# Layer norm's two small operations moved from GpSimd to VectorE, with six reorderings in a fused attention and FFN kernel

## What is computed

```
xn = layernorm(x)
q, k, v = xn @ Wq.T, xn @ Wk.T, xn @ Wv.T        # 16 heads of 16
q, k    = q / |q|, k / |k|                       # per head
p       = softmax(q k.T - slope_h * |distance|)  # only the next 127 keys and the own one
s       = (p v) @ Wo.T
gate    = fp4(xn) @ fp4(w_gate).T                # 256 -> 704; fp4 in blocks of 16
h       = silu(gate) * (fp4(xn) @ fp4(w_up).T)
g       = silu(fp4(h) @ fp4(w_down).T)           # 704 -> 256
out     = x + s * g
```

## Time and profile before

| | us |
|---|---|
| median of three runs | 502.65 |
| the profiled execution | 503.14 |
| its span in the profile | 501.4 |
| TensorE busy | 451.2 (90%) |
| VectorE busy | 441.2 (88%) |
| GpSimd busy | 409.6 (82%) |
| ScalarE busy | 402.5 (80%) |
| one turn of the loop (silu's start to silu's next start, 233.13 to 247.19) | 14.06 |

### The profile page before, as it was taken

How to read it: one execution, slowest core, us unless ns; L and a number is a source line. 1 busy time by engine, 2 the same in 40 slices (tenths; PEclk the granted TensorE clock), 3 DMA queues, 4 the chain that set the end, 5 groups by cost and what they waited for, 6 DMA issues and landing times.

```text
span 501.4 us, 14045 instructions
## 1 busy us (share of the span) xinstructions
PE 451.2 (90%) x4990; PEld 314.2 (63%) x4990; DVE 441.2 (88%) x897; ACT 402.5 (80%) x584; POOL 409.6 (82%) x897
## 2 busy tenths in 40 slices
PE   0378889999999999999999999999999999999997
PEld 0144556666667666676767676667666766666665
DVE  4989989999989999989989999988998999887686
ACT  1466988988888888888887888888888888888952
POOL 6544678899988888889997898989999888887751
PEclk9857999999999999999999999999999999999999
DMA  8211011224321314223221222222422121222100
GB/s 300 88 43 44 6 37 44 65 75 76 75 63 45 45 41 67 64 64 64 66 65 43 64 34 54 65 54 54 54 54 54 44 24 43 54 54 54 44 22 33
DMA packets 78276, 29.35 MB, mean 59 GB/s; under 512 B 67712, under 2 KB 77696, under 8 KB 78208
## 3 DMA queue, kind: packets, MB, share of 16 engines
q1 hardware_dynamic: 77920, 28.39, 24.7%
q10 hardware_dynamic: 288, 0.08, 0.1%
HBM read 7.49 MB, written 4.19 MB: 23 GB/s over the span
## 4 chain that ended last, share of the span: by engine, by line
PE 53%; ACT 20%; issue 11%; DVE 10%; POOL 3%; DMA 1%; ACTq 0%; DVEq 0%; POOLq 0%
PE gt L351 10%; PE up L351 10%; PE gt L551 9%; ACT probs L1341 8%; PE bank_q L351 8%; PE bank_b L357 5%; ACT L1341 4%; PE gt L573 4%; ACT pv_t L1219 3%; ACT qk_sq L1319 3%; PE bank_b L598 2%; PE scores L505 2%; PE gt L555 1%; DMA qk_slots<-qk_stack 1%; PE gt L357 1%
## 5 line engine op out<-in xcount | busy, mean ns | idle before, releaser
L1341 ACT ACTIVATE probs<-scores 128x1024 f32<-128x1024 f32 (+1 forms) x101 | 102.2, 1012 | 2.3 <-PE scores L505 1.2
L1526 POOL TENSOR_SCALAR_AFFINE_SELECT probs<-probs 128x512 f32<-128x512 f32 x128 | 81.9, 641 | 1.7 <-ACT probs L1341 1.3
L1533 POOL TENSOR_SCALAR_AFFINE_SELECT probs<-probs 128x512 f32<-128x512 f32 x120 | 76.2, 637 | 3.7
L598 PE MATMUL bank_b<-probs,vals 128*32 128x128 f32 x1952 | 59.7, 274 | 0.6 <-DVE vals L944 0.3
L598 PEld LDWEIGHTS bank_b<-probs,vals 128*32 128x32 f32 x1952 | 51.6, 110 | 7.4 <-issue 5.7
L1219 ACT ACTIVATE qk_stack<-bank_q 128x512 f16<-128x512 f32 x64 | 35.1, 595 | 22.3 <-DVE bank_q L923 22.3
L793 DVE SCALAR_TENSOR_TENSOR xT_lo<-gt,xT_hi 128x512 f16<-128x512 f32 (+1 forms) x34 | 22.3, 657 | 26.3 <-ACT xT_hi L1219 26.3
L551 PE MATMUL gt<-wdn_hi,hT_hi 128*128 128x256 f16 x160 | 43.6, 273 | 0.6 <-DVE hT_lo L845 0.6
L551 PE MATMUL gt<-wdn_hi,hT_lo 128*128 128x256 f16 x160 | 43.6, 273 | 0.0
L551 PE MATMUL gt<-wdn_lo,hT_hi 128*128 128x256 f16 x160 | 43.6, 273 | 0.0
L1563 POOL TENSOR_TENSOR h_q<-h_grid,h_scale 128x704 f32<-128x704 bf16 x31 | 43.1, 1391 | 0.0
(11 more groups left out here) (219 smaller groups left out, 1468.5 us busy)
## 6 DMA issues: line engine op xcount, KB each, us to landing
out<-y SPq DMA_DIRECT2D x32, 128.0 KB, 1.9
x_all<-x SPq DMA_DIRECT2D x20, 128.0 KB, 2.0
x_all<-x SPq DMA_DIRECT2D x3, 512.0 KB, 4.1
x_all<-wproj SPq DMA_DIRECT2D x1, 768.0 KB, 6.9
dn_raw<-wd SPq DMA_DIRECT2D x1, 704.0 KB, 8.7
probs<-wg SPq DMA_DIRECT2D x1, 640.0 KB, 5.3
probs<-wu SPq DMA_DIRECT2D x1, 640.0 KB, 7.6
qk_slots<-qk_stack SPq DMA_TRANSPOSE x32, 3.7
```

Of the source, the lines that this page charges most:

```text
L598: done = e.matmul(pv_bank(i)[32 * n:32 * n + 32, grp * P:(grp + 1) * P], va, pr, start=part == 0, stop=part == 1 or final(i))
L1341: e.activation(probs[j % P_BUFS][:, grp, :, side(j), :], score_banks(j, grp)[:, :, :, side(j), :].rearrange("p b e h q -> p (b e) h q"), A ...
L1526: e.affine_select(out=own, in_=own, compare_op=ALU.is_ge, fill=0.0, base=0, pattern=[[0, GRP], [-1, P]], channel_multiplier=1).then_inc(s_ ...
L1533: e.affine_select(out=part, in_=part, compare_op=ALU.is_gt, fill=0.0, base=0, pattern=[[0, GRP], [1, P]], channel_multiplier=-1).then_inc( ...
```

## The change

`ln_parts`, two operations on one column, goes from GpSimd to VectorE, behind `denom`. In the loop, six things change place: scores of the first four heads ahead of tr_x (TensorE); norm_x ahead of lo_x, and hidden ahead of unit (VectorE); hi_x between the first and the second exp (ScalarE).

```diff
@@ tensor_program
             for t in range(4, 31):
+                scores(t - 1, 0)
                 tr_x(t + 1)
-                scores(t - 1, 0)
                 scores(t - 1, 1)
@@ vector_program
+            def ln_parts(t):
+                e.wait_ge(s_moments, t + 1)
+                if t >= 2:
+                    e.wait_ge(s_rs, roots(t - 3, Z_ARG))
+                    e.wait_ge(s_xn, t)
+                e.tensor_scalar(ss[:, ln_col(t)], moments[:, 1:2], LN_EPS, None, ALU.add).then_inc(s_var, 1)
+                e.tensor_scalar(mean_col(t), moments[:, 0:1], -1.0, None, ALU.mult).then_inc(s_neg_mean, 1)
...
             denom(0)
+            ln_parts(6)
             attend(0)
...
                 rscale_x(t + 1)
+                norm_x(t + 1)
                 lo_x(t + 1)
...
+                hidden(t - 2)
                 unit(t)
-                hidden(t - 2)
                 gated(t - 4)
...
                 denom(t - 3)
-                norm_x(t + 1)
+                if exists(t + 3):
+                    ln_parts(t + 3)
                 attend(t - 3)
@@ scalar_program
                 exp(t, 0)
+                hi_x(t + 2)
                 exp(t, 1)
                 keep_pv(t - 2)
-                hi_x(t + 2)
                 hi_h(t - 2)
@@ gpsimd_program
                 mask_own(t - 2, 3)
-                if exists(t + 2):
-                    ln_parts(t + 2)
                 mask_prev(t - 2, 3)
```

## The result

The changed kernel takes 535.92 us in the median of six runs (532.62 to 542.09), the kernel before 502.76; the ratio is 1.0655 (1.0632 to 1.0678). It is slower, as forecast, but by 33 us where 21 were forecast, and the time lies outside the range of 514 to 530. The execution that was profiled is the slowest of the six, 542.09 us with a span of 540.4, and the ratio is that of the other five, whose median is 535.62.

What follows compares the result with a forecast made beforehand. A ring over ScalarE and TensorE bounds the kernel at 14.06 us a turn; the change makes a longer ring, 26 x 0.80 = 20.8 us, plus 0.48, together 21.3: 524.0 us, range 514 to 530.

Steps and rivals of the forecast that it cites:

- Ring A: Silu, exps, keep_pv on ScalarE, then TensorE's tr_tail to gate products: sets the 14.06 us turn; hi_x makes it 14.54.
- Ring B: From silu over keep_pv, up product, hidden, unit, hi_q, lo_qk, norm_h, square_h to silu: turn of 14.86 us, 0.80 more.
- rival 1: Only ring A counts, hidden's wait finding unseen slack: turn of 14.54 us, 516 us in all; chance 0.11.
- Ln_parts: Move from GpSimd to VectorE: 0.46 us for the pair on VectorE, no gain from GpSimd's relief.
- rival 2: Ln_parts is slow on VectorE beside the masks, at 1.2 us a turn of 15.2 us: 532 us; chance 0.09.
- Norm_x ahead of lo_x: On VectorE: norm_x takes 0.3 of some 0.9 us to spare at lo_x, so effect 0.
- Scores ahead of tr_x: On TensorE: scores fill the 0.28 us wait for silu, but nothing on either ring moves, so effect 0.
- its room: TensorE's free time between the scores' wait for the transposes and tr_tail, taken as about 0.7 us.
- the sum: Whole-run total: 26 x 0.80 = 20.8 us plus 0.48 behind the last turn, 21.3 us more; 524.0 us.
- a floor: The slow 0.60 us of L884, taken as upper bound for each ln_parts operation on VectorE, 1.2 for the pair.
- the short ring: Ring A, over ScalarE and TensorE, forecast at 14.54 us with hi_x in it.
- the long one: Ring B, going on over VectorE's hidden and unit back to silu, forecast at 14.86 us.

Runs made afterwards that it cites:

- a_unit_first: The changed kernel with unit ahead of hidden again: 515.48 us, ratio 1.0251.
- a_tr_x_first: The changed kernel with tr_x ahead of the scores again: 528.72 us, ratio 1.0518.
- the kernel without newest transposes: The changed kernel, its loop scores reading q and k of the tile before, so no transpose is waited for: 528.36 us, ratio 1.0512.
- a_tr_x_first_late: The changed kernel with tr_x ahead of the scores and the q and k transposes issued 1.5 us later: 530.54 us, ratio 1.0555.
- a_hi_x_back: The changed kernel with hi_x behind keep_pv again: 531.11 us, spread from 519.95 to 533.46, no ratio given.

## Why the prediction was wrong

- *Ring A is the turn, and hi_x lengthens it by 0.48.* Right. The copy alone gives 514.86, and with unit first the clean turn is the forecast 14.54.
- *Ring B through hidden and unit.* Right in every place, small by 0.12 us a turn: 14.98 instead of 14.86. The product was ready at 8.02, but hidden started at 8.13 and not at 8.06; lo_qk started 0.11 behind the end of hi_k and not 0.03, at 10.85 instead of 10.67. Against that stands a shorter pitch of square_x (0.30). Silu has no wait for TensorE, so rival 1 is out. Over 26 turns that is 3 us.
- *Ln_parts.* Right, and cheaper than taken: 0.24 for the pair against 0.46, so rival 2 is out. The Trainium skill's rule of contention on the shared SBUF interfaces (GPSIMD Engine Reference, Key points) did not touch these two: 0.10 and 0.14 us in each of 26 turns, beside a mask of GpSimd in the three turns looked at.
- *Norm_x ahead of lo_x: 0.* No run has it alone, and none disputes it: with the two costly edits undone 1 to 2 us are left, which turns behind late transposes account for.
- *Scores ahead of tr_x: 0.* **This is the step that failed.** I saw the danger (the transposes must have landed) and worked it out with the one median of the earlier trace rows, 3.7 us. The kernel before already had seven of 4.7 to 5.6 us, which cost it nothing, since its scores asked some 5.5 us after lo_qk. In the changed kernel lo_qk ends 1.55 us later in the turn (11.54 instead of 9.99) and the scores ask first, 3.84 us after the issue (152.25 to 156.09), so each such transpose kept TensorE waiting for 1.35 to 2.56 us. That is beyond its room, which I had put at 0.7 us and which was 1.1. And the wait took the clock with it, which I hadn't in the sum. Measured: 7.5 us in the median run, where the sum had 0. It takes both orders: with unit first (a_unit_first) or with tr_x first (a_tr_x_first) late transposes cost next to nothing.
- *The range.* 14.98 alone gives 528.4, as the kernel without newest transposes shows, inside 514 to 530. The late transposes put the time outside.

Which waits are followed by the lower clock is left open. In the two executions of the changed kernel none of the six waits of 1.21 to 1.54 us was, and eleven of the twelve of 1.55 to 2.56 us were, all but one of 1.86. In other kernels one of 1.19 us was (a_tr_x_first_late) and one of 1.67 was not (a_hi_x_back), so the length of the wait alone does not decide. Also open is whose instructions q8 loads, and why such a load slows a transpose; only that they fall together, and that moving the issue ends it, was shown.

## What to carry to other kernels

When an edit eats into the slack ahead of a DMA, read the spread of its landing times turn by turn, not the median: a transfer that is late in every fourth turn is free as long as there is slack, and then, here, cost its lateness beyond the slack and the TensorE clock behind it. When a step is moved ahead of another on an in-order engine, write down what it waits for and follow everything queued behind it once around the loop; ring lengths from starts in one turn's timeline came within 0.01 us for the short ring and 0.12 for the long one. Filling an idle gap off the ring that closes the turn was worth nothing here (504.21 us with the scores first, 502.61 without).

## What the runs showed that was not expected

- A DMA transpose of q and k takes 3.6 to 4.1 us to land in nearly three turns of four and 4.3 to 6.4 in the others; in 14 executions 100 of 101 such late ones had an instruction load start within 2.8 us of their issue.
- Issuing it 1.5 us later made the late ones of 5 us and more vanish in all three kernels that tried it.
- Behind a wait of 1.7 us the 64 small products took 3.25 us instead of 1.95, at a mean granted clock of 0.90 in that turn.
- The maximum with a constant over 32 columns on VectorE (L884 before, L892 after; the prediction calls it a floor), 600 ns in the median beside GpSimd's q_h, takes 321 ns in the changed kernel. It ends with q_h in both (236.19 and 236.16 us before, 252.30 and 252.25 after), but starts later in the second. In all 27 turns of either trace in which it stands beside q_h it ends 0.03 to 0.04 us behind it, whatever its length (0.32 to 0.95 us); in the three of either trace with nothing of GpSimd beside it, it takes 0.17 us. So the 600 ns that the prediction took as a price are the rest of q_h's time from its start:

```profile
L892 DVE TENSOR_SCALAR ss<-ss x32: 168/321/646, 20.1 to 498.9; 128x32 f32<-128x32 f32 x32
```
